# Softmax attention of block 0 with a second, transposed score product

## The chip, the cores and the metric

One core of a Trainium2 chip runs the kernel. Its engines work side by side and wait for one another by semaphores: TensorE (PE, with its weight loads as PEld), VectorE (DVE), ScalarE (ACT), GpSimd (POOL), and SyncE (SP), which issues most transfers. The metric is the time of one execution in microseconds (us). The kernel before takes 4012.47 us, the median of 3 runs (4009.18 to 4015.44). A difference of 0.2%, 8 us, is about what a measurement of this kernel can tell from no change.

## The reference

64 sequences of 128 tokens, width 256, go through two transformer blocks. The change is in the two attentions of the first block ("block 0"): 16 heads of width 16, one self-attention and one cross-attention over 128 context rows of width 192.

```python
def _attn(q, k, v):          # 16 heads of 16
    scores = jnp.einsum('bhnd,bhmd->bhnm', q, k) * HD ** (-0.5)
    p = jax.nn.softmax(scores, axis=-1)
    return jnp.einsum('bhnm,bhmd->bhnd', p, v)      # then heads joined

h = _ln(x, ln1_w, ln1_b) * (1 + sc1) + sh1
q, k, v = jnp.split(h @ Wqkv + bqkv, 3, axis=-1)
x = x + _attn(q, k, v) @ Wos + bos
h = _ln(x, ln2_w, ln2_b) * (1 + sc2) + sh2
x = x + _attn(h @ Wq + bq, context @ Wk + bk, context @ Wv + bv) @ Woc + boc
h = _ln(x, ln3_w, ln3_b) * (1 + sc3) + sh3
x = x + gelu(h @ W1 + b1) @ W2 + b2
...                          # block 1: two attentions with heads of 64, one FFN
```

## The kernel before

**Passes and ticks.** The work is six passes over all 64 sequences: two attentions of block 0 (kind "a", passes 0 and 1), its FFN (pass 2), two attentions of block 1 (kind "b", passes 3 and 4), its FFN (pass 5). Within a pass the sequences go in 16 groups of 4; one sequence is called a batch here. The function `schedule` (L127) puts every stage of every batch at a tick, a step of an imaginary clock that all engines go through in the same order. Each engine's program is one loop over the ticks, and within a tick it runs its stages in the order in which the code has them. So the order on each engine is fixed; how long a tick lasts is up to the waits. Passes 0 and 1 take 4 ticks a batch, 16 a group.

**fp32r triples.** Products that need fp32 accuracy are made of three fp32r products (`three`, L617 to L624): each operand is split into a high part (rounded to fp32r) and a low part, and high x high, high x low and low x high add up in one PSUM bank. Products of plain fp32 operands are written as one `matmul`; the trace shows each as two MATMUL records.

**One batch in passes 0 and 1.** q and k of a group are projected with head and channel on the partitions (L705, L713) and split: AH and AL for q, KBH and KBL for k; k is stored twice, times a mask that keeps one head of each pair. The heads lie in four row groups of 32 partitions. `scores0` (L690 to L703) makes, for one half of a batch (two row groups), twelve fp32r products of 256 columns, with queries on the partitions of the result, in PSUM banks 0 and 1 or 2 and 3. The DVE takes the maxima (`max0`, L1065). ACT computes exp(score - max) with the maximum as its per-partition bias and sums each row by the way (`exp0`, L926): 16 instructions of 128 columns a batch, each with an accumulator read. The DVE takes 1/sum (L1078), POOL multiplies (`normal`, L1265), PE turns each of the four tiles with four transposes (`p_turn`, L816), and DVE (three tiles, L1073) and ACT (one, L958) copy them into PT. Then `pv0` (L748) multiplies with V, ACT and DVE split the result into OH and OL (L917, L1125), and `out0` makes the output projection, which `res0` (L1106) adds to X.

**PSUM.** Banks 0 to 3 hold the scores. Everything else takes turns through banks 4 to 7 (`Banks`, L89): each use waits until the use before it in that bank has been read.

**Names.** `s_s0` counts score halves, `s_nm0` maxima, `s_exp` exponentials, `s_t` turned tiles, `s_ol` split outputs. `q.wait_ge(semaphore, value)` makes an engine wait.

## Time and profile before

| | before |
|---|---|
| median of 3 runs | 4012.47 us |
| the profiled execution | 4010.95 us |
| its span, first to last instruction | 4009.1 us |
| PE, DVE, ACT, POOL busy | 3839.5, 3157.0, 2468.4, 2862.1 us (96, 79, 62, 71%) |
| granted TensorE clock, mean | 0.993 |

The table's busy shares are means over six passes of three kinds. Passes 0 and 1 end near 1200 us, the FFN of block 0 near 1560 us, block 1's attentions near 3620 us. A stage is read from windows that lie wholly inside it. L numbers are lines of the kernel before. PE records have modelled ends: a matmul's duration contains a tail that the next one overlaps, so what a group of matmuls costs is read from its start to the start of what follows.

### The profile page before, as it was taken

How to read it: one execution, taken by the hardware profiler on the slowest of the kernel's cores; microseconds unless marked ns; L12 is line 12 of the kernel's file. 1: busy time of each engine (PE TensorE's matmuls, PEld its weight loads, DVE VectorE, ACT ScalarE, POOL GpSimd, SP SyncE). 2: the span in 40 equal slices, each digit the busy share in tenths (PEclk: the TensorE clock that was granted, in tenths of full speed). 3: DMA queues.
4: the chain of work that ended last, by engine and by line, in shares of the span. 5: the costliest groups of instructions: out<-in, count | busy, mean ns of one | idle time of the engine just before them, and what ended most of it. 6: DMA issues, size and time to landing. Idle time of an engine off the chain costs nothing.

```text
span 4009.1 us, 92934 instructions
## 1 busy us (share of the span) xinstructions
PE 3839.5 (96%) x32822; PEld 3295.7 (82%) x32822; DVE 3157.0 (79%) x6610; ACT 2468.4 (62%) x10244; POOL 2862.1 (71%) x2674
## 2 busy tenths in 40 slices
PE   7999999999989999999999999899999999999999
PEld 6777777777779997888888888788888888878998
DVE  7888889899985557888888888799998999975443
ACT  6999998898883334555555555455555555554333
POOL 5777877777767777666666666577777777766776
PEclk9999999999999999999999999999999999999999
DMA  2011111111111123777767677777777777772110
GB/s 81 28 33 33 33 46 41 41 49 49 54 40 54 43 64 102 219 210 219 216 212 223 208 222 225 215 213 235 223 231 222 226 231 225 231 227 85 52 43 32
DMA packets 415216, 544.98 MB, mean 136 GB/s; under 512 B 58524, under 2 KB 311968, under 8 KB 414752
## 3 DMA queue, kind: packets, MB, share of 16 engines
q1 hardware_dynamic: 267228, 404.74, 30.7%
q10 hardware_dynamic: 147524, 134.30, 12.9%
q8 instruction: 261, 4.28, 0.5%
q14 instruction: 203, 1.66, 0.1%
HBM read 220.11 MB, written 184.55 MB: 101 GB/s over the span
## 4 chain that ended last, share of the span: by engine, by line
PE 69%; DVE 12%; ACT 8%; DMA 4%; issue 3%; POOL 3%; ACTq 1%; SPq 0%; DVEq 0%
PE BANKS L621 17%; PE BANKS L622 15%; PE BANKS L623 15%; PE BANKS L780 6%; PE BANKS L768 5%; ACT PR L926 5%; PE BANKS L701 3%; PE BANKS L816 3%; DMA PB<-p_scratch 2%; DMA p_scratch<-TR 2%; PE BANKS L838 2%; DVE WL L1118 1%; DVE PT L1073 1%; POOL PR L1265 1%; DVE SN L1146 1%
## 5 line engine op out<-in xcount | busy, mean ns | idle before, releaser
L1265 POOL TENSOR_TENSOR PR<-PR,RL 128x512 f32<-128x512 f32 x1024 | 1064.1, 1042 | 602.9 <-DVE RL L1078 602.5
L942 ACT ACTIVATE PR<-BANKS,NM 128x128 f32<-128x128 f32 x2048 | 719.3, 378 | 334.5 <-DVE NM L1132 333.9
L926 ACT ACTIVATE PR<-BANKS,NM 128x128 f32<-128x128 f32 x2048 | 728.7, 414 | 12.7 <-DVE NM L1065 10.5
L621 PE MATMUL BANKS<-HH,WH 128*128 128x512 f32 x1632 | 681.4, 418 | 9.1 <-issue 7.4
L622 PE MATMUL BANKS<-HL,WH 128*128 128x512 f32 x1632 | 643.4, 394 | 0.0
L623 PE MATMUL BANKS<-HH,WL 128*128 128x512 f32 x1632 | 642.5, 394 | 0.0
L926 ACT ACTIVATION_READ_ACCUMULATOR PR<-BANKS,NM 128x1 f32 x2048 | 521.3, 255 | 0.0
L933 ACT ACTIVATE OH<-BANKS 128x512 fp32r<-128x512 f32 x256 | 153.1, 598 | 499.6 <-PE BANKS L768 257.8
L1132 DVE TENSOR_REDUCE NM<-BANKS 128x8 f32<-128x1024 f32 x256 | 310.4, 1213 | 190.4 <-PE BANKS L780 190.3
L942 ACT ACTIVATION_READ_ACCUMULATOR PR<-BANKS,NM 128x1 f32 x2048 | 445.5, 218 | 0.0
L621 PE MATMUL BANKS<-WH,OH 128*128 128x256 f32 x1280 | 375.6, 293 | 25.0 <-DVE OL L1150 20.8
L1277 POOL TENSOR_TENSOR HL<-HF,HH 128x512 fp32r<-128x512 f32 x192 | 256.3, 1335 | 171.0 <-DVE HH L1026 157.0
L621 PEld LDWEIGHTS BANKS<-HH,WH 128*128 128x128 f32 x1632 | 308.4, 189 | 84.1 <-issue 11.1
L969 ACT ACTIVATE HF<-BANKS,MODB,MODS 128x128 f32<-128x128 f32 x768 | 305.4, 487 | 115.5 <-PE BANKS L838 104.4
L816 PE MATMUL BANKS<-ID,PR 128*128 128x128 f32 x2048 | 316.9, 278 | 57.5 <-DVE OL L1125 22.0
L623 PEld LDWEIGHTS BANKS<-HH,WL 128*128 128x128 f32 x1632 | 308.3, 189 | 69.2
L622 PE MATMUL BANKS<-WL,OH 128*128 128x256 f32 x1280 | 359.9, 281 | 0.0
L1073 DVE COPY PT<-BANKS 128x512 f32<-128x512 f32 x384 | 262.9, 685 | 122.1 <-PE BANKS L816 121.0
L623 PE MATMUL BANKS<-WH,OL 128*128 128x256 f32 x1280 | 359.1, 281 | 0.0
L1085 DVE STREAM_TRANSPOSE TR<-PR 128x512 f32<-128x512 f32 x512 | 348.5, 681 | 10.3 <-POOL PR L1265 10.3
L1146 DVE TENSOR_TENSOR SN<-BANKS,ROPE 128x512 f32<-128x512 f32 x512 | 346.9, 677 | 6.1 <-DMA SW<-SN 5.9
L622 PEld LDWEIGHTS BANKS<-HL,WH 128*128 128x128 f32 x1632 | 309.3, 189 | 43.8
(134 smaller groups left out, 10692.2 us busy)
## 6 DMA issues: line engine op xcount, KB each, us to landing
SW<-SN SPq DMA_DIRECT2D x1024, 128.0 KB, 2.9
p_scratch<-TR SPq DMA_DIRECT2D x256, 512.0 KB, 4.7
PB<-p_scratch ACTq DMA_DIRECT2D x1024, 128.0 KB, 3.8
x_scratch<-X SPq DMA_DIRECT2D x80, 512.0 KB, 3.2
X<-x_scratch SPq DMA_DIRECT2D x80, 512.0 KB, 4.3
CX<-in_ctx SPq DMA_DIRECT2D x32, 384.0 KB, 4.4
X<-in_x SPq DMA_DIRECT2D x16, 512.0 KB, 4.0
out<-X SPq DMA_DIRECT2D x16, 512.0 KB, 2.9
```

The costliest lines, as they stand in the source:

```text
L621: e.matmul(o, lh, rh, start=first and i == 0, stop=False)
L622: e.matmul(o, lh, rl, start=False, stop=False)
L623: made = e.matmul(o, ll, rh, start=False, stop=last and i == n - 1)
L816: made = e.transpose(bank[:, 128 * h:128 * h + 128], PR[npr(t)[0]][:, 128 * h:128 * h + 128], ID[:, :])
L926: made = e.activation(pr[:, r], bank[:, r], ACT.Exp, bias=nm[:, h:h + 1], accum_out=RL[npr(t)[0]][:, h:h + 1])
L942: made = e.activation(pr[:, r], bank[:, r], ACT.Exp, bias=nm[:, h:h + 1], accum_out=RL[npr(t)[0]][:, h:h + 1])
L969: made = e.activation(HF[u % 2][:, x.c, r], bank[:, r], ACT.Identity, bias=MODB[:, s, x.c, bb:bb + 1], scale=MODS[:, s, x.c, bb:bb + 1])
L1073: e.tensor_copy(PT[npt(t)[0]][:, :], PS[tp.bank(("p", t.n))][:, :]).then_inc(s_pt_d, 1)
L1085: e.transpose(TR[i % NTR][:, :].rearrange("p (j k c) -> p j k c", j=4, k=8)[:, :, 4 * e_:4 * e_ + 4, :], PR[npr(t)[0]][:, :].rearrange("p ...
L1132: e.tensor_reduce(NM[x.i % 2][:, :], BANKS[:, 2:4, :].rearrange("p e (h k) -> p (e h) k", h=4), AX, ALU.max, negate=True).then_inc(s_nm, 1)
L1146: e.tensor_tensor(SN[r % 2][:, :].rearrange("p (b t) -> p b t", b=G), src, sn, ALU.mult).then_inc(s_rt, 1)
L1265: e.tensor_tensor(p3, p3, RL[npr(t)[0]][:, :].unsqueeze(2).broadcast_to([128, 4, 128]), ALU.mult).then_inc(s_nrm, 1)
```

## The change

Passes 0 and 1 compute their softmax in another way; block 1 and the FFNs stay as they are.

- **Operands.** q and k are no longer split. QB is q times the mask (twice, one for each head of a pair), KF is k, both plain fp32. The bias of k is added by ACT (the products with BK and ONES are gone).
- **First score product, for the maxima.** `scores` makes eight plain fp32 products of 128 columns a half, always in banks 0 and 1.
- **The maxima get onto the partitions that are contracted.** POOL splits the 16 maxima of a batch into high and low (`top`), PE turns them in one transpose (`top_turn`), and the DVE spreads them with a mask into M (`top_out`).
- **Second score product.** Six ticks later `turned_scores` makes the same scores with keys on the partitions (four plain fp32 products of 256 columns a half, banks 2 and 3), and `turned_tops` adds minus the maximum through four fp32r products of 256 columns with a matrix of zeros and ones (SEL). On PE both halves are issued as one block: the scores of one half and the turned scores of another half, which always lies in the other two row groups.
- **exp** is then one ACT instruction of 512 columns per tile, four a batch, without bias and sum, and writes PT itself. `normal`, `p_turn` and the PT copies are gone.
- **Sums.** The unused columns of V hold 1.0 instead of 0.0, so `pv0` (same count of products, now each with its own output columns) also gives each head's sum. The DVE transposes the result in 32x32 blocks (`sums`) and takes the reciprocals, POOL scales it (`scale0`, two instructions), the DVE transposes it back (`back`), ACT and POOL split it (`high0`, `low0`).
- **Ticks.** `pv0` comes 10 ticks after the batch's first score tick instead of 8 (and the first score tick is 2 later), `out0` 15 instead of 10. Group loads, norms, turns, q and k are later, nearer to their use. Three empty ticks stand between passes 1 and 2, and W2 is split later.

```diff
-                for stage, tick in (("v", tb - 3), ("v_out", tb - 2), ("pv0", tb + 8), ("high0", tb + 9), ("low0", tb + 9),
-                                    ("out0", tb + 10), ("res0", tb + 11)):
-                for u in range(4):
-                    for stage, lag in (("exp0", 0), ("normal", 1), ("p_turn", 3), ("p_copy", 4)):
+                for h in range(2):
+                    for stage, lag in (("scores0", 0), ("max0", 1), ("turned0", 6), ("exp0", 7)):
+                        at[stage, tb + 2 * h + lag].append(y)
+                for stage, lag in (("v", -3), ("v_out", -2), ("top", 4), ("top_turn", 5), ("top_out", 5), ("pv0", 10), ("sums", 11), ("scale0", 12),
+                                   ("back", 13), ("high0", 13), ("low0", 14), ("out0", 15), ("res0", 16)):
...
+            def scores(x, c, e_):
+                for r in (2 * x.h, 2 * x.h + 1):
+                    rows = slice(32 * r, 32 * r + 32)
+                    made = e.matmul(PS[r % 2][:, 256 * c + 128 * e_:256 * c + 128 * e_ + 128], QB[ga % 2][rows, c, e_, s], KF[ga % 2][rows, c, s],
+                                    start=True, stop=True)
+            def turned_scores(y, c):
+                for r in (2 * y.h, 2 * y.h + 1):
+                    e.matmul(PS[2 + r % 2][:, 256 * c:256 * c + 256].rearrange("p (e n) -> p e n", e=2), KF[ga % 2][rows, c, s], QB[ga % 2][rows, c, :, s],
+                             start=c == 0, stop=False)
+            def turned_tops(y, c):
+                    made = e.matmul(PS[2 + r % 2][:, 256 * c:256 * c + 256].rearrange("p (e n) -> p e n", e=2), SEL[rows, c, :], M[y.i // 2 % 2][rows, :, :],
+                                    start=False, stop=c == 1)
...
-                    q.wait_ge(s_exp, 4 * (4 * ga + x.b) + 2 * x.h - 2)
-                        for k, (qt, kt) in enumerate(((AH, KBH), (AH, KBL), (AL, KBH))):
-                                made = e.matmul(PS[r][:, 256 * c:256 * c + 256].rearrange("p (e n) -> p e n", e=2), qt[ga % 2][rows, c, s],
-                                                kt[ga % 2][rows, c, :, s], start=k == 0, stop=k == 2)
+                    q.wait_ge(s_nm0, x.i)
+                for y in turned:
+                    q.wait_ge(s_m, y.i // 2 + 1)
+                    q.wait_ge(s_exp, 2 * y.i)
+                for c in range(2):
+                    for x in halves:
+                        scores(x, c, 0)
+                    for y in turned:
+                        turned_scores(y, c)
+                    for x in halves:
+                        made = scores(x, c, 1)
...
-                for t in at["p_turn", tick]:
-                        made = e.transpose(bank[:, 128 * h:128 * h + 128], PR[npr(t)[0]][:, 128 * h:128 * h + 128], ID[:, :])
...
-                        made = e.activation(pr[:, r], bank[:, r], ACT.Exp, bias=nm[:, h:h + 1], accum_out=RL[npr(t)[0]][:, h:h + 1])
+                    for r in (2 * x.h, 2 * x.h + 1):
+                        e.activation(PT[(4 * (x.i // 2) + r) % NPT0][:, :], PS[2 + r % 2][:, :], ACT.Exp).then_inc(s_exp, 1)
...
+                    e.transpose(TO[vi % 2][:, :, :, :, :].rearrange("p c e q d -> p (c e q d)"), PS[tp.bank(("pv", x))][:, :]).then_inc(s_to, 1)
+                        made = e.reciprocal(RC[vi % 2][:, :, e_, :], TO[vi % 2][:, :, e_, :, 16 - 16 * e_])
...
+                    e.tensor_tensor(M[vi % 2][:, :, :], PS[tp.bank(("top", x))][:, 0:128].unsqueeze(1).broadcast_to([128, 2, 128]),
+                                    MASK[:, 2:4].unsqueeze(2).broadcast_to([128, 2, 128]), ALU.mult).then_inc(s_m, 1)
...
+                    e.tensor_copy(top[:, :, 0:4], nm).then_inc(s_toph, 1)
+                    e.tensor_tensor(top[:, :, 4:8], nm, top[:, :, 0:4].bitcast(F), ALU.subtract).then_inc(s_topl, 1)
```

On PE, in a tick with a score half of pass 1, before (HH.. are projections; L701 scores, L748 `pv0`, L816 `p_turn`):

```order
L701 MATMUL BANKS<-WH,AH 128x256 x2
L701 MATMUL BANKS<-WL,AH 128x256 x2
L701 MATMUL BANKS<-WH,AL 128x256 x2
L748 MATMUL BANKS<-PT,V 32x128 [waits s_res,s_pt_a]
L748 MATMUL BANKS<-PT,V 32x128 x15
L816 MATMUL BANKS<-ID,PR 128x128 [waits s_nrm]
```

The same place after (L666 scores, L675 turned scores, L682 the maxima's products, L743 `pv0`; QBH is the buffer of QB, s_m tells that M is there):

```order
L666 MATMUL BANKS<-KF,QBH 128x128 [waits s_exp,s_m,s_nm0]
L666 MATMUL BANKS<-KF,QBH 128x128
L675 MATMUL BANKS<-QBH,KF 128x256 x2
L666 MATMUL BANKS<-KF,QBH 128x128 x4
L675 MATMUL BANKS<-QBH,KF 128x256 x2
L666 MATMUL BANKS<-KF,QBH 128x128 x2
L682 MATMUL BANKS<-M,SEL 128x256 x4
L743 MATMUL BANKS<-PT,V 32x128 [waits s_res]
L743 MATMUL BANKS<-PT,V 32x128 x15
```

The transposes behind `pv0` are gone, and the block in front of it holds two kinds of fp32 products in turn, with one set of waits ahead of all.

On DVE, two ticks of pass 1 before (L1065 maxima, L1073 PT copy, L1125 split of the output, L1097 V):

```order
L1065 TENSOR_REDUCE NM_1<-BANKS 128x8 [waits s_s0]
L1073 COPY PT<-BANKS 128x512 [waits s_t]
L1078 RECIPROCAL RL<-RL 128x4 [waits s_exp]
L1125 TENSOR_TENSOR OL<-BANKS,OH 128x256 [waits s_oh]
L1073 COPY PT<-BANKS 128x512 [waits s_pv0,s_t]
```

And after (L1079 maxima, L1086 and L1103 block transposes, L1136 residual, L1096 M):

```order
L1079 TENSOR_REDUCE NM_1<-BANKS 128x8 [waits s_s0]
L1086 STREAM_TRANSPOSE TO<-BANKS 128x512 [waits s_pv0]
L1089 RECIPROCAL RC<-TO 128x2x4 [waits s_to]
L1089 RECIPROCAL RC<-TO 128x2x4
L1136 TENSOR_TENSOR X<-BANKS,X 128x256 [waits s_bias,s_y]
L1079 TENSOR_REDUCE NM_0<-BANKS 128x8 [waits s_topl,s_s0]
L1096 TENSOR_TENSOR M<-BANKS,MASK 128x256 [waits s_ts,s_tt]
L1103 STREAM_TRANSPOSE OF<-NO 128x256 [waits s_ol,s_no]
```

The copies of PT are gone; M is made right behind the maxima of the next batch's first half.

## Rows read from the trace of the kernel before

**Rows 1.** Windows: PE, PEld, DVE, ACT, POOL busy us (instructions), clock, DMA share, GB/s.
```profile
255.10:533.90 278.80, 262.19 (x2962) 221.59 (x2961) 236.66 (x545) 258.16 (x1203) 221.38 (x225) 1.00 0.10 32
750.80:1039.50 288.70, 264.14 (x2978) 221.96 (x2977) 261.82 (x586) 259.09 (x1203) 221.30 (x225) 1.00 0.15 45
1240.00:1560.00 320.00, 317.70 (x2068) 288.07 (x2067) 170.09 (x368) 117.26 (x224) 235.21 (x205) 1.00 0.18 58
```

**Rows 2.** Waits in 255.1 to 533.9: waiter, cause, total us, times, longest us.
```profile
PEld BANKS L701 <- ACT PR L926: 11.7, 24, 0.7
```

**Rows 3.** Timeline of PE, 402 to 411 us: start, duration, what, count.
```profile
402.32 0.60 PE L816 MATMUL BANKS<-ID,PR 128*128 128x128 f32 x4
402.68 0.48 PE L621 MATMUL BANKS<-HH,WH 128*128 128x512 f32 x1
...
404.15 0.60 PE L816 MATMUL BANKS<-ID,PR 128*128 128x128 f32 x4
404.68 0.38 PE L701 MATMUL BANKS<-WH,AH 32*128 32x256 f32 x2
...
405.58 1.08 PE L748 MATMUL BANKS<-PT,V 128*32 128x128 f32 x32
406.59 0.66 PE L816 MATMUL BANKS<-ID,PR 128*128 128x128 f32 x4
407.00 0.37 PE L621 MATMUL BANKS<-WH,HH 128*128 128x256 f32 x1
...
407.80 0.60 PE L816 MATMUL BANKS<-ID,PR 128*128 128x128 f32 x4
408.55 0.39 PE L701 MATMUL BANKS<-WH,AH 32*128 32x256 f32 x2 [0.15 <-ACT PR L926]
...
410.63 0.48 PE L723 MATMUL BANKS<-ONES,BK 128*128 128x512 f32 x1
410.95 0.40 PE L621 MATMUL BANKS<-HH,WH 128*128 128x512 f32 x1
```

**Rows 4.** Timeline of PE near 2002 us, block 1's plain fp32 scores.
```profile
2001.59 1.16 PE L780 MATMUL BANKS<-KT,QT 64*128 64x128 f32 x16
2002.68 0.50 PE L621 MATMUL BANKS<-HH,WH 128*128 128x512 f32 x1
```

**Rows 5.** Timeline of PE near 36.7 us, the first two score halves.
```profile
36.63 0.38 PE L701 MATMUL BANKS<-WH,AH 32*128 32x256 f32 x4
36.85 0.28 PE L701 MATMUL BANKS<-WL,AH 32*128 32x256 f32 x4
36.97 0.28 PE L701 MATMUL BANKS<-WH,AL 32*128 32x256 f32 x4
```

**Rows 6.** Groups by line, 255.1 to 533.9 us: busy us, mean ns | idle before.
```profile
L926 ACT ACTIVATE PR<-BANKS,NM 128x128 f32<-128x128 f32 x514 | 182.8, 413 | 0.0
L1265 POOL TENSOR_TENSOR PR<-PR,RL 128x512 f32<-128x512 f32 x129 | 133.9, 1044 | 56.8 <-DVE RL L1078 56.8
L1065 DVE TENSOR_REDUCE NM<-BANKS 128x8 f32<-128x1024 f32 x64 | 77.5, 1211 | 0.0
L1073 DVE COPY PT<-BANKS 128x512 f32<-128x512 f32 x96 | 65.9, 686 | 39.7 <-PE BANKS L816 39.1
L1324 POOL TENSOR_TENSOR X<-X,TB 128x256 f32<-128x256 f32 x32 | 23.6, 738 | 0.0
L1118 DVE SCALAR_TENSOR_TENSOR WL<-BANKS,MASK,WH 128x512 fp32r<-128x512 f32 x32 | 22.5, 746 | 1.4
L1078 DVE RECIPROCAL RL<-RL 128x4 f32<-128x4 f32 x128 | 21.4, 167 | 0.0
L1300 POOL TENSOR_TENSOR RS<-VE,MH 128x4 f32<-128x4 f32 x8 | 8.3, 1037 | 0.7
```

**Rows 7.** Groups by line, DVE, 1600 to 3600 us: block 1's 32x32 block transposes.
```profile
L1085 DVE STREAM_TRANSPOSE TR<-PR 128x512 f32<-128x512 f32 x500 | 340.4, 681 | 10.3 <-POOL PR L1265 10.3
```

**Rows 8.** Groups by line, ACT, from 1400 us: the FFN's Gelu from PSUM.
```profile
L985 ACT ACTIVATE GF<-BANKS,COL 128x512 f32<-128x512 f32 x55 | 37.9, 689 | 102.2 <-PE BANKS L623 102.2
```

338 lines of the change are left out of this document (173 added, 165 removed).

## The prediction

> **What bounds the kernel now.** I read the windows first. In a steady stretch of pass 0 (32 batches, 278.8 us, so 8.71 us a batch) ACT is busy 258.16 us, 93%, and PE 262.19 us, 94%; POOL has 79%, DVE 85%. In pass 1 (32 batches in 288.7 us, 9.02 us a batch) PE has 91%, DVE 91% and ACT 90%: three engines in lockstep. In the FFN PE reaches 99% (317.7 of 320 us) [rows 1]. Then the waits: PE's score weights wait for ACT's exponentials, 11.7 us in 24 waits of the pass 0 stretch [rows 2]. So in pass 0 ACT sets the pace, with PE close behind. Two passes of 64 batches are 128 x 8.87 = 1135 us; that is all that the change can touch, 28% of the span.
>
> **What PE loses.** From its start to the start of what follows, a turned tile (L816) takes 402.68 - 402.32 = 0.36, 404.68 - 404.15 = 0.53, 407.00 - 406.59 = 0.41 and 408.55 - 407.80 less 0.15 idle = 0.60 us [rows 3]: 1.90 us a batch. The bias product L723 takes 410.95 - 410.63 = 0.32, one for two batches: 0.16. A score half (L701) takes 405.58 - 404.68 = 0.90; two are 1.80. Together 3.86. PE's busy time a batch is 262.19/32 = 8.19 in pass 0 and 264.14/32 = 8.25 in pass 1 [rows 1]; 4.33 and 4.39 stay.
>
> **What PE gets.** The price of plain fp32 stands in block 1: eight products of 128 columns in two row groups (16 records, L780) take 2002.68 - 2001.59 = 1.09 us to the next start [rows 4]. Of this about 0.2 is the change-over to the next kind of product: L701's twelve products go out in six pairs 0.12 apart (36.97 after 36.85), 0.70, and need 0.90 [rows 3, 5]. So eight plain products are 0.89. The new block has exactly eight of 128 columns in two row groups, and four of 256 columns, the same work, in the other two: 0.89 each, and four fp32r products of 256 columns, two pairs at 0.12, 0.23. Do the two 0.89 lie beside each other? Rows 5 answer this: the first two halves' products start four at a time, at 36.63, 36.85 and 36.97, two of each half. The program has all twelve of the second half behind the first half's twelve, yet its first ones start beside the seventh and eighth. Row groups run as streams of their own, and a stream that is behind doesn't hold up the others. The block then costs 0.89 + 0.23 + 0.2 = 1.33 (sum 1.32, rounded up), 2.66 a batch. Its other end is no overlap at all: 0.89 + 0.89 + 0.23 + 0.2 = 2.21, 4.42 a batch. I take 1.33: rows 5 show the same row groups and banks in fp32r. The turned maxima are one transpose: 0.09 (a quarter of the shortest group) to 0.6 (a whole group), I take 0.26. `pv0` keeps its 16 products (1.01 us, 405.58 to 406.59 [rows 3]). The kept 4.33 plus 2.92 is 7.25 a batch in pass 0, and 7.31 in pass 1.
>
> The Trainium skill, page "TensorE: Matmul & The Clock Gate", section "Part 3: Packing small matmuls - row/col tiling", has products of different row groups run together but says that matmuls start and end strictly in program order. By that rule the alternating short and long products of the block could hold one another up. The trace disagrees where it can be seen (36.63, rows 5); what the rule would make of the block is the first rival below.
>
> **The other engines.** ACT: L926's 182.8/32 = 5.7 us a batch go (its accumulator reads too), and one PT copy [rows 6]; four exponentials of 512 columns, one and a half q and k copies at 0.69 each [rows 8] come, 3.8, against two such copies before. 8.07 becomes about 5: far from the bound. DVE: 236.66/32 = 7.40, less three PT copies (65.9/32 = 2.06), two k splits (0.70) and four reciprocals (0.67) [rows 1, 6] is 3.97; to come are a 512-column transpose at 0.68 [rows 7], one of 256 (half, 0.35), M (256 columns from PSUM, half of a 0.69 copy and a start, 0.4) and two small reciprocals (0.33): 1.8, so 5.8; in pass 1 8.18 becomes 6.6. The transpose reads PSUM, which L1085 doesn't: L1073 reads 512 columns of PSUM in 0.686, so I add nothing. POOL: 6.92 less L1265's 4.18 is 2.74 [rows 1, 6]. To come are the two small `top` instructions, two scalings of 128 columns and a split of 256. 256 columns cost 0.738 and 512 cost 1.044 [rows 6], a line with 0.43 at zero and 0.58 at 128: 0.43 x 2 + 0.58 x 2 + 0.85 for the split (between the two rows) = 2.9, in sum 5.6. No row shows a strided scaling or so small a copy; the upper end is 1.04 for each of the five (as L1300, 4 elements): 7.9. So PE is the bound, and it is the only engine near it.
>
> **Waits that come in.** Ahead of a block PE waits for the maxima of the half before (s_nm0), for M and for the exponentials. Everything on PE stands behind it: `pv0`, projections, turns. In a tick pair with M: maxima 1.21 us [rows 6] and a hop of 0.2, then M 0.4 and a hop, about 1.95 after the first scores end. PE has, until the next block, the maxima's products (0.23), the transpose, v (0.8, 407.00 to 407.80 [rows 3]) and in three batches of four a q, k or turn: 1.3 us alone, 1.7 to 2.7 with those. So one or two waits of a few tenths a group. With exponentials: 2 x 0.69 and a hop, 1.6, behind at least 1.8 of work in the other tick pair. The hop of 0.2 is an estimate, of the size of PE's change-over. I allow 0.3 us idle a batch in pass 0 and 0.4 in pass 1, where DVE has 86%; before it was 8.71 - 8.19 = 0.52 and 0.77. The periods become 7.55 and 7.71.
>
> **The sum.** Pass 0: (8.71 - 7.55) x 64 = 74 us. Pass 1: (9.02 - 7.71) x 64 = 84 us. The way through a batch is longer (15 ticks to `out0`, not 12), and three empty ticks precede the FFN; W2's split and two Gelu rows come between the last exponentials. The last batch's chain after its scores (two blocks, four exponentials, `pv0`, DVE, POOL, DVE, ACT, POOL, about 11 us by the prices above) is covered in part by the first FFN products: I add 8 us, between 0 and 20. Span 4009.1 - 158 + 8 = 3859; around it lie 4010.95 - 4009.1 = 1.9 us, so 3861. The median of the runs is 1.5 above the profiled execution: **3862 us**.
>
> Bounds of this case: if the block's change-over costs nothing (0.4 a batch less) and PE idles only as in the FFN (1%), a batch takes 6.92 and 6.98, so 245 us go instead of 158: 3775. If idle stays as before (0.52 and 0.77, 0.3 more on the mean) and each block costs 0.3 more: 3862 + 128 x 0.3 + 128 x 0.6 = 3977.
>
> **Rivals.**
> - *No overlap in the block* (slower). Place: the alternation L666, L675 on PE. A block costs 2.21; a batch 4.33 + 4.42 + 0.26 + 0.1 idle = 9.11 in pass 0 and 9.17 in pass 1, which is 0.40 and 0.15 more than before: so 4012 + 35 + 8 = 4055. It decides from a block of about 1.95 us on ((8.71 - 4.33 - 0.26 - 0.2)/2). For it: no row shows plain fp32 in four row groups, nor unequal lengths beside each other. Against it: rows 5. This is the result that the page's rule gives.
> - *POOL becomes the bound.* With its upper end, 7.94 busy and 0.2 idle, 8.14 a batch, (0.57 + 0.88) x 64 = 93 us go and 8 come: 4012 - 85 = 3927. For it: L1300's 4 elements take 1.04 [rows 6]. Against: that is one operation (a power), all others shrink with size.
> - *The change doesn't shorten the stage because the chains do the pacing*: score, maxima, M, next block. If each tick pair took 1.95 + 1.33 + 1.0 of delay by DVE's order, a batch takes 8.6, 1.0 more than forecast: 3862 + 128 = 3990, hardly faster. For it: DVE runs `back` and M in order behind the maxima, and `back` waits for POOL. Against: DVE has 14% or more free.
>
> **Chances.** Forecast case 0.75; POOL 0.08; chains 0.07; no overlap 0.08; the rest (something between the blocks' two ends, near 4012) 0.02. The range 3780 to 3970 holds most of the forecast case (its own bounds are 3775 and 3977) and the POOL case, and leaves out the chain's and the slower one. Faster by over 0.2% (8 us, what a measurement can tell): 0.89; within: 0.03; slower: 0.08.
>
> **What would show it.** In a timeline of PE, L666 and L675 records start together (four at a time) and the block from first start to `pv0` takes about 1.3 us; 2.2 would be the rival. Windows inside pass 0 should give PE about 95% and ACT about 65%, with 7.5 us a batch. POOL at 70 to 75%, its small instructions at 0.3 to 0.6 us; `top` at 1 us would speak for the second rival. DVE's L1086 at 0.7 us. A wait of PE for DVE's M over 0.5 us a batch would show the chain. Block 1 and the FFNs must keep their times; a change there would be an error of this reading.

## The result and the profile after

The changed kernel takes 3900.89 us (median of 4 runs, 3897.50 to 3902.93), the one before 4013.95 us beside it: ratio 0.9716, interval 0.9698 to 0.9733. Forecast were 3862 us and a range of 3780 to 3970. The sign and the range held; 39 us of the forecast gain did not come. The profiled execution took 3901.6 us, its span is 3899.6 us.

The span cut at the starts of the same records in both traces (the maxima, L1079 after and L1065 before, and the Gelus, L999 after and L985 before) shows where:

| stage | before | after | change | forecast |
|---|---|---|---|---|
| start to first maximum | 41.77 | 39.86 | -1.9 | 0 |
| pass 0: to the 129th maximum | 563.10 | 483.42 | -79.7 | -74 |
| pass 1: to the last maximum | 570.66 | 513.42 | -57.2 | -84 |
| change-over: to the 17th Gelu | 60.06 | 77.38 | +17.3 | +8 |
| FFN, 96 Gelus | 278.96 | 282.32 | +3.4 | 0 |
| block 1: to the 129th Gelu | 2110.95 | 2115.21 | +4.3 | 0 |
| second FFN, to the end | 383.62 | 388.00 | +4.4 | 0 |

Windows of the changed kernel, 32 batches of pass 0, 32 of pass 1, and FFN; they answer to [rows 1], with the same columns (PE, PEld, DVE, ACT, POOL busy, clock, DMA share, GB/s):
```profile
222.30:460.20 237.90, 230.34 (x3492) 194.19 (x3488) 181.94 (x400) 138.49 (x272) 150.78 (x257) 1.00 0.13 39
653.70:915.50 261.80, 240.76 (x3508) 200.42 (x3504) 207.17 (x441) 140.26 (x272) 150.63 (x257) 0.97 0.17 50
1130.00:1316.00 186.00, 186.00 (x1205) 169.67 (x1204) 93.40 (x211) 65.79 (x127) 133.84 (x119) 1.00 0.14 46
```
In pass 0 a batch takes 237.90/32 = 7.43 us, PE is busy 97% of it and ACT 58%, no longer 93%. Pass 1 is another picture: 8.18 us a batch, PE at 92%, and a mean clock of 0.97.

The block itself, in the timeline of PE (start, duration, what, count, idle before it):
```profile
402.40 0.38 PE L666 MATMUL BANKS<-KF,QBH 32*128 32x128 f32 x2
402.42 0.48 PE L675 MATMUL BANKS<-QBL,KF 32*128 32x256 f32 x2
402.59 0.42 PE L666 MATMUL BANKS<-KF,QBH 32*128 32x128 f32 x4
...
403.20 0.47 PE L682 MATMUL BANKS<-M,SEL 32*128 32x256 f32 x2
403.26 0.30 PE L666 MATMUL BANKS<-KF,QBH 32*128 32x128 f32 x2
403.50 0.28 PE L682 MATMUL BANKS<-M,SEL 32*128 32x256 f32 x2
403.85 1.08 PE L743 MATMUL BANKS<-PT,V 128*32 128x128 f32 x32
```
Scores (L666) and turned scores (L675) start 0.02 apart and run beside each other. This one takes 1.45 us to the start of `pv0`. Of the 43 blocks between 260 and 420 us the median is 1.31 us from the first start to the start of what follows; forecast was 1.33.

Groups by line in the same stretch of pass 0 (busy us, mean ns | idle before), which answer to [rows 6] and [rows 7]:
```profile
L1079 DVE TENSOR_REDUCE NM<-BANKS 128x8 f32<-128x1024 f32 x64 | 78.1, 1221 | 28.4 <-PE BANKS L666 28.3
L923 ACT ACTIVATE PT<-BANKS 128x512 f32<-128x512 f32 x128 | 69.6, 597 | 59.7 <-PE BANKS L682 59.7
L1287 POOL TENSOR_TENSOR NO<-TO,RC 128x128 f32<-128x128 f32 x64 | 24.5, 403 | 7.9 <-DVE RC L1089 7.9
L1295 POOL TENSOR_TENSOR OL<-OF,OH 128x256 fp32r<-128x256 f32 x32 | 23.4, 730 | 39.5 <-ACT OH L947 39.5
L1086 DVE STREAM_TRANSPOSE TO<-BANKS 128x512 f32<-128x512 f32 x32 | 22.9, 715 | 1.3
L1096 DVE TENSOR_TENSOR M<-BANKS,MASK 128x256 fp32r<-128x256 f32 x32 | 13.4, 420 | 14.3 <-PE BANKS L751 14.3
L1280 POOL TENSOR_TENSOR TOP<-NM,TOP 128x16 fp32r<-128x16 f32 x32 | 7.2, 225 | 2.6
L1278 POOL CAST TOP<-NM 128x16 fp32r<-128x16 f32 x32 | 6.4, 200 | 10.8 <-DVE NM L1079 10.8
```
ACT's exponentials went from 182.8 us [rows 6] to 69.6, and they now wait for PE. POOL's two small `top` instructions cost 0.20 and 0.23 us, not 0.43 and never 1.04, so the rival in which POOL is the bound has nothing left: POOL has 150.78/32 = 4.7 us a batch, forecast were 5.6.

What is wrong in pass 1 stands once in every group in the timeline of PE:
```profile
785.13 0.28 PE L639 MATMUL BANKS<-WL,HH 128*128 128x256 f32 x1
786.85 0.44 PE L860 MATMUL BANKS<-ID,Z 128*128 128x128 f32 x2 [1.45 <-ACT HF L982]
787.60 0.66 PE L871 MATMUL BANKS<-ID,CX 128*128 128x128 f32 x4 [0.31 <-DVE HL L1232]
...
790.26 1.92 PE L743 MATMUL BANKS<-PT,V 128*32 128x128 f32 x32
```
A `turn` waits 1.45 us until ACT has read another one out of its PSUM bank, a `c_turn` 0.31 for DVE. ACT is late by the new chain: in its timeline the read (L982) stands behind `high0` (L947), and this one has waited for DVE's `back` (L1103).
```profile
785.69 0.42 ACT L947 ACTIVATE OH<-OF 128x256 fp32r<-128x256 f32 x1 [0.66 <-DVE OF L1103]
786.01 0.79 ACT L982 ACTIVATE HF<-BANKS,MODB,MODS 128x128 f32<-128x128 f32 x2
```
All twelve such waits between 600 and 1000 us have these 0.66 us in front. Behind PE's two waits, `pv0` takes 1.85 us to the next start (792.11) where it took 1.01 in [rows 3]. The windows ahead of the waits and behind them (columns as above):
```profile
776.00:785.00 9.00, 9.00 (x141) 7.78 (x138) 6.33 (x13) 5.95 (x12) 4.54 (x10) 1.00 0.37 121
788.60:792.10 3.50, 3.50 (x58) 2.73 (x50) 2.30 (x3) 1.08 (x2) 0.34 (x1) 0.51 0.57 150
```
PE was busy without a gap at a granted clock of 1.00, stood for 1.45 + 0.31 = 1.8 us with 0.44 of work between, and went on; from 788.5 on the granted clock fell, and each of the three microseconds from 789 to 792 has 0.50, the lower of the two levels.

At the change-over from pass 1 to the FFN, PE stands still before the FFN's first `down` (the second product of the FFN; `up` is the first). Timeline of ACT, DVE and PE:
```profile
1059.17 1.28 ACT L923 ACT_TABLE_LOAD   x1
1060.46 1.08 ACT L923 ACTIVATE PT<-BANKS 128x512 f32<-128x512 f32 x2
...
1061.87 1.28 ACT L999 ACT_TABLE_LOAD   x1
...
1063.75 1.99 ACT L1005 ACTIVATE WH<-STG 128x1024 fp32r<-128x1024 f32 x2
...
1064.83 3.57 DVE L1260 TENSOR_TENSOR WL<-STG,WH 128x1024 fp32r<-128x1024 f32 x2 [0.52 <-ACT WH L1005]
...
1068.51 0.55 PE L614 MATMUL BANKS<-WH,GH 128*128 128x256 f32 x1 [8.25 <-DVE WL L1260]
```
By the last row W2's low part, behind two changes of ACT's function table, is what `down` waits for, 8.25 us.

### The profile page after: what moved, and what is told of

It is laid out like the page before. It is cut to its first block, busy times and chain, and to the rows that moved or that the text cites. A ratio compares the mean times of both kernels' runs of the same rounds, so it can differ in the third digit from the quotient of the medians.

```text
span 3899.6 us, 92972 instructions
## 1 busy us (share of the span) xinstructions
PE 3750.1 (96%) x34934; PEld 3217.8 (83%) x34934; DVE 2930.1 (75%) x6035; ACT 1996.6 (51%) x6534; POOL 2583.4 (66%) x2803
## 4 chain that ended last, share of the span: by engine, by line
PE 79%; DVE 9%; issue 4%; POOL 3%; DMA 2%; ACT 1%; ACTq 1%; SPq 0%; DVEq 0%; POOLq 0%
PE BANKS L614 19%; PE BANKS L615 17%; PE BANKS L616 17%; PE BANKS L810 6%; PE BANKS L798 6%; PE BANKS L666 3%; PE BANKS L743 2%; PE BANKS L675 2%; POOL HL L1313 2%; PE BANKS L860 2%; PE BANKS L682 1%; DMA p_scratch<-TR 1%; DVE SN L1156 1%; DMA PB<-p_scratch 1%; PE BANKS L626 1%
## 5 line engine op out<-in xcount | busy, mean ns | idle before, releaser
L962 ACT ACTIVATE PR<-BANKS,NM 128x128 f32<-128x128 f32 x2048 | 720.9, 379 | 348.3 <-DVE NM L1142 348.0
L1301 POOL TENSOR_TENSOR PR<-PR,RL 128x512 f32<-128x512 f32 x512 | 533.0, 1041 | 335.8 <-DVE RL L1108 334.9
L1142 DVE TENSOR_REDUCE NM<-BANKS 128x8 f32<-128x1024 f32 x256 | 310.3, 1212 | 197.2 <-PE BANKS L810 197.1
L962 ACT ACTIVATION_READ_ACCUMULATOR PR<-BANKS,NM 128x1 f32 x2048 | 444.7, 217 | 0.0
L923 ACT ACTIVATE PT<-BANKS 128x512 f32<-128x512 f32 x512 | 278.3, 596 | 279.8 <-PE BANKS L682 279.1
L1079 DVE TENSOR_REDUCE NM<-BANKS 128x8 f32<-128x1024 f32 x256 | 312.7, 1221 | 108.3 <-PE BANKS L666 107.4
L982 ACT ACTIVATE HF<-BANKS,MODB,MODS 128x128 f32<-128x128 f32 x768 | 293.5, 457 | 138.8 <-PE BANKS L860 134.7
L1308 POOL TENSOR_TENSOR QT<-QT,SW 128x512 f32<-128x512 f32 x256 | 332.5, 1299 | 10.4 <-DMA SW<-SN 10.4
L1308 POOL TENSOR_TENSOR KT<-KT,SW 128x512 f32<-128x512 f32 x256 | 330.7, 1292 | 13.0 <-DMA SW<-SN 12.7
```

The lines of the kernel that those rows point to most:

```text
L962: made = e.activation(pr[:, r], bank[:, r], ACT.Exp, bias=nm[:, h:h + 1], accum_out=RL[npr(t)][:, h:h + 1])
L982: made = e.activation(HF[u % 2][:, x.c, r], bank[:, r], ACT.Identity, bias=MODB[:, s, x.c, bb:bb + 1], scale=MODS[:, s, x.c, bb:bb + 1])
L1079: e.tensor_reduce(NM0[x.i // 2 % 2][:, x.h, :, :], BANKS[:, 0:2, :].rearrange("p r (h k) -> p r h k", h=4), AX, ALU.max, negate=True).then ...
L1142: e.tensor_reduce(NM[x.i % 2][:, :], BANKS[:, 2:4, :].rearrange("p e (h k) -> p (e h) k", h=4), AX, ALU.max, negate=True).then_inc(s_nm, 1)
L1301: e.tensor_tensor(p3, p3, RL[npr(t)][:, :].unsqueeze(2).broadcast_to([128, 4, 128]), ALU.mult).then_inc(s_nrm, 1)
L1308: e.tensor_tensor(z[:, :], z[:, :], SW[r % NSW][:, :], ALU.add).then_inc(s_zz, 1)
```

## The experiments

All times are medians; "less" and "more" are against the changed kernel's 3900.9 us unless said otherwise. Ratios with their intervals are to the kernel before, run beside them (4009 to 4012 us).

**Why the block overlaps.** The changed kernel issues two score products, then two turned ones, and so on. Three runs change this order and nothing else, and a fourth adds a wait to it.

All score products first (16 records of L666), then all turned ones:
```diff
-                for c in range(2):
-                    for x in halves:
-                        scores(x, c, 0)
-                    for y in turned:
-                        turned_scores(y, c)
-                    for x in halves:
-                        made = scores(x, c, 1)
-                        if c == 1:
-                            made.then_inc(s_s0, 1)
+                for x in halves:
+                    for c in range(2):
+                        scores(x, c, 0)
+                        made = scores(x, c, 1)
+                    made.then_inc(s_s0, 1)
+                for c in range(2):
+                    for y in turned:
+                        turned_scores(y, c)
```


> The changed kernel with one thing moved: PE issues all eight score products of a half first, then the four turned products, then the tops, instead of one pair in turn with the other. Waits, products and sizes are the same. Theory (row groups run as streams of their own; a product of an idle row group starts although longer ones stand ahead of it): the block still takes about 1.45 us from its first start to pv0's, the run is within 0.3% of the changed kernel's 3900.9 us. Rival A (products start strictly in program order, and only the alternation gave the overlap): the turned ones start only when the last score product has started, about 0.7 us later, so the block takes 1.9 to 2.2 us, x 256 blocks = 120 to 190 us more: 4020 to 4090 us. Rival B (it overlaps, but the maxima can start earlier since the scores all stand ahead): up to 0.1 us a block less, 3875 to 3900 us, visible in pass 1 above all.

Measured: 4019.2 us (4014.2 to 4024.9), ratio 1.0021 (1.0009 to 1.0032): the whole gain is gone. One block in the timeline of PE (L859 is what follows):
```profile
405.75 0.82 PE L666 MATMUL BANKS<-KF,QBL 32*128 32x128 f32 x10
406.32 0.48 PE L675 MATMUL BANKS<-QBH,KF 32*128 32x256 f32 x2
406.42 0.39 PE L666 MATMUL BANKS<-KF,QBL 32*128 32x128 f32 x4
...
407.10 0.59 PE L682 MATMUL BANKS<-M,SEL 32*128 32x256 f32 x4
407.61 0.44 PE L859 MATMUL BANKS<-ID,Z 128*128 128x128 f32 x2
```
The first turned records start when ten score records have started and six have not, 0.56 us late; the block takes 407.61 - 405.75 = 1.86 us. My theory is wrong as it stands, and so is rival A, by which they would have waited for all sixteen.

All score products first, and PE waits until they are done (the edit as it stands on top of the run just shown):
```diff
+                    q.wait_ge(s_s0, x.i + 1)
                 for c in range(2):
                     for y in turned:
                         turned_scores(y, c)
```


> The changed kernel, all score products of a half first, and PE then waits for their completion before it issues the turned products, so nothing in the block overlaps. This is the price of no overlap. By the prediction's terms (0.89 more a block) the block takes 2.2 to 2.4 us, 256 x 0.8 to 0.95 = 205 to 243 us more, less where PE would have waited anyway (0.24 us a batch in pass 0, 0.66 in pass 1, 115 us at most): 4000 to 4140 us, 4090 us taken. If it comes out below 3950 us, the overlap isn't what holds the block at 1.45 us, and something else sets the block's time.

Measured: 4236.4 us (4230.1 to 4242.1), ratio 1.0566 (1.0551 to 1.0582), 335 more. In its timeline of PE:
```profile
405.10 1.16 PE L666 MATMUL BANKS<-KF,QBL 32*128 32x128 f32 x16
406.32 1.13 PE L675 MATMUL BANKS<-QBL,KF 32*128 32x256 f32 x8
407.11 0.58 PE L682 MATMUL BANKS<-M,SEL 32*128 32x256 f32 x4
407.62 0.33 PE L751 MATMUL BANKS<-ID,TOP 128*128 128x128 f32 x1
```
The block takes 2.52 us, 1.21 more than 1.31. I had it at 2.2 to 2.4: the turned ones start 1.22 after the first score product, not 0.89, since a wait for completion also sees the last product's 0.27 us to its end. 256 x 1.21 = 310 us is near the 335 by luck. Pass 0 takes 134 us more than in the changed kernel, less than 128 x 1.21 = 155, for PE's idle time shrank; pass 1 takes 206 more, 11.5 us a batch, at a mean granted clock of 0.87 (720 to 1300 us).

Coarser steps: for each c four score products (8 records), then the two turned ones.
```diff
                 for c in range(2):
                     for x in halves:
                         scores(x, c, 0)
+                        made = scores(x, c, 1)
+                        if c == 1:
+                            made.then_inc(s_s0, 1)
                     for y in turned:
                         turned_scores(y, c)
-                    for x in halves:
-                        made = scores(x, c, 1)
-                        if c == 1:
-                            made.then_inc(s_s0, 1)
```


> The changed kernel with the block's products alternating in coarser steps: for each c, first the four score products (8 records), then the two turned ones (4 records). In the run with all score products ahead (4019.2 us, 16 records ahead) the turned ones started 0.56 us after the block's start, when 10 of the 16 score records had started and 6 were still to come. Theory (a product of an idle row group may pass about six records that have not started, and no more): here only 6 records are left ahead when the first pair has started, so the turned ones start within 0.12 us of the block's start; the block takes 1.45 to 1.55 us, the run 3895 to 3925 us. Rival (a product passes only its next neighbour or two, and the time depends on how fine the alternation is): the turned ones start 0.3 us late in each c, the block takes 1.65 to 1.8 us, the run 3950 to 3990 us.

Measured: 3918.4 us (3912.1 to 3923.6), ratio 0.9764 (0.9748 to 0.9780). The turned ones start 0.03 us after the first two score records, with six ahead; the median block takes 1.43 us. The theory had 1.45 to 1.55 us and a run of 3895 to 3925.

Twelve records ahead, to test the number:
```diff
+                for x in halves:
+                    scores(x, 0, 0)
+                    scores(x, 0, 1)
+                    scores(x, 1, 0)
+                for y in turned:
+                    turned_scores(y, 0)
+                for x in halves:
+                    scores(x, 1, 1).then_inc(s_s0, 1)
+                for y in turned:
+                    turned_scores(y, 1)
```


> The changed kernel with twelve score records ahead of the first turned product in each block (then four turned records, the last four score records, the last four turned ones). It tests the look-ahead by number. Theory (a record of an idle row group starts once no more than six that have not started stand ahead): the turned ones start with the seventh and eighth score record, 0.33 us after the block's start, in the run with sixteen ahead it was with the ninth and tenth, 0.56; the block takes 1.63 us (1.31 in the changed kernel), the run 3950 to 3980 us. Rival A (the look-ahead covers a fixed time, about 0.6 us, and not a number of records): the turned ones start at 0.56 here too, or at 0. Rival B (a coarser alternation costs nothing as long as it alternates): block below 1.45 us, run below 3925.

Measured: 3963.8 us (3956.7 to 3967.8), ratio 0.9882 (0.9864 to 0.9901), block 1.63 us. In its timeline of PE:
```profile
405.50 0.60 PE L666 MATMUL BANKS<-KF,QBL 32*128 32x128 f32 x6
405.84 0.48 PE L675 MATMUL BANKS<-QBL,KF 32*128 32x256 f32 x2
```
Six score records have started when the turned ones start, at 0.34 us: six are left again. All three numbers are as expected. It is a number of records and not a fixed time. The four orders give blocks of 1.31, 1.43, 1.63 and 1.86 us and 3901, 3918, 3964 and 4019 us.

The Trainium skill, page "TensorE: Matmul & The Clock Gate", section "Part 3: Packing small matmuls - row/col tiling", has matmuls start strictly in program order. The records disagree: a pair of L675 at 406.32 starts ahead of six records of L666 that stand before it in the program. The reach is six records. It stood in the trace of the kernel before, just ahead of [rows 5]:
```profile
36.28 0.39 PE L701 MATMUL BANKS<-WH,AH 32*128 32x256 f32 x2
36.50 0.28 PE L701 MATMUL BANKS<-WL,AH 32*128 32x256 f32 x2
36.62 0.28 PE L701 MATMUL BANKS<-WH,AL 32*128 32x256 f32 x2
```
Six of the first half's twelve records had started when the second half's first pair did, at 36.63 (the pair with 0.38 us among those four; the first half's own next pair came at 36.73). Six were left there too. Those products are fp32r, one record each, and the plain fp32 ones have two, so the reach counts records and not products. I had read the rows as having no such limit.

**Who held the kernel before, ACT or PE.** First the kernel before with ACT relieved alone:
```diff
-                    for h in range(4):
-                        r = slice(128 * h, 128 * h + 128)
-                        made = e.activation(pr[:, r], bank[:, r], ACT.Exp, bias=nm[:, h:h + 1], accum_out=RL[npr(t)[0]][:, h:h + 1])
-                    made.then_inc(s_exp, 1)
+                    e.activation(pr[:, :], bank[:, :], ACT.Exp, scale=0.01).then_inc(s_exp, 1)
```


> The kernel before with ACT relieved alone: each tile's four exponentials of 128 columns with row sums become one of 512 columns without maxima and sums (left out: the maxima, the sums, and a scale of 0.01 keeps the numbers finite; the sums are ones from a fill). PE, DVE and POOL do all that they did. ACT falls from 8.07 to about 5.1 us a batch. Theory (of the prediction: PE is right behind ACT, with 8.19 to 8.25 us of busy time a batch, so ACT's relief alone is worth little, and the rest of the gain is PE's shorter work): a batch takes 8.35 to 8.6 us in both passes, so 3940 to 3985 us, a third of the change's gain at most. Rival (ACT set the pace alone, and its relief is the whole gain): 3900 us or less, 7.4 to 7.8 us a batch. Second rival (DVE and POOL in lockstep hold it): 3995 to 4010 us, no gain.

Measured: 3991.4 us (3988.4 to 3993.3), ratio 0.9948 (0.9932 to 0.9965): 20 us of 113. Its window in pass 0:
```profile
255.00:530.00 275.00, 263.86 (x2964) 222.07 (x2964) 236.13 (x545) 153.66 (x305) 221.94 (x225) 1.00 0.10 32
```
This run leaves out the maxima and the row sums of the exponentials. ACT fell to 56%, PE went from 94 to 96%, and a batch from 8.71 to 8.59 us. So in pass 0 ACT was first by little, and PE next, as the prediction said. In pass 1 a batch fell from 9.04 to 8.88 us (48 batches each) and not to 8.6; PE had 93% there and DVE 92%, so there DVE's part, the second rival, isn't ruled out. The time lies 6 us above the theory's range and 4 below this rival's.

Then the other corner, the changed kernel with dearer exponentials:
```diff
-                        e.activation(PT[(4 * (x.i // 2) + r) % NPT0][:, :], PS[2 + r % 2][:, :], ACT.Exp).then_inc(s_exp, 1)
+                        pt, bank = PT[(4 * (x.i // 2) + r) % NPT0], PS[2 + r % 2]
+                        for k in range(4):
+                            s = slice(128 * k, 128 * k + 128)
+                            made = e.activation(pt[:, s], bank[:, s], ACT.Exp, accum_out=SUM[:, 4 * r + k:4 * r + k + 1])
+                        made.then_inc(s_exp, 1)
```


> The changed kernel with ACT's exponentials as dear as in the kernel before: each of 512 columns is cut into four of 128 with a row sum (into a spare tile that nobody reads), about 5.7 us a batch instead of 2.2; PE, DVE and POOL do what the changed kernel does. With the run that relieved ACT alone (3991.4 us, 20 less than before) this is the other corner. Theory (both are needed: before, ACT's 8.07 and PE's 8.2 us a batch stood side by side, so either cut alone is worth little): ACT is at 7.8 to 8.1 us a batch, a batch of pass 0 takes 8.0 to 8.3 us, of pass 1 8.3 to 8.6, the run 3940 to 3985 us. Rival (PE alone was the bound and ACT only looked like it): within 10 us of the changed kernel's 3900.9. The spare tile moves the FFN's buffers by another 64 bytes; whether its 16 down units take 46.5 or 47.05 us shows which places are the slow ones, at most 12 us of the run.

Measured: 3930.7 us (3928.5 to 3935.1), ratio 0.9807 (0.9792 to 0.9822), below the expected 3940 to 3985. Its window in pass 0, with ACT busy in the fourth place:
```profile
222.00:464.00 242.00, 224.65 (x3391) 189.48 (x3386) 177.44 (x391) 195.31 (x1134) 144.94 (x249) 1.00 0.11 37
```
ACT got only to 81%, 6.3 us a batch and not the 8 that I had meant, for without the maxima as bias an exponential took 0.295 us. So the run doesn't build the corner that it was for. Still passes 0 and 1 together took 503.35 + 540.33 = 1043.7 us against 996.8: 47 us more although ACT was not the busiest engine. The rival, within 10 us, falls: the cut on PE is worth less with ACT loaded so far. How much a fully loaded ACT would cost stays open, and with it whether the gain needs both cuts. Part of the 47 us was given back further on (below).

**Pass 1.** The context's transposes two ticks later, out of the tick in which `turn`, `top_turn` and `v` take banks too:
```diff
-                    at["c_turn", tg - 16 + c if p == 1 else tg - 7].append(Part(p, g, c, 0))
+                    at["c_turn", tg - 14 + c if p == 1 else tg - 7].append(Part(p, g, c, 0))
-                    at["c_split", tg - 15 + c if p == 1 else tg - 6].append(Part(p, g, c, 0))
+                    at["c_split", tg - 13 + c if p == 1 else tg - 6].append(Part(p, g, c, 0))
```


> The changed kernel with the transposes of the context (c_turn, pass 1) two ticks later, at tg-14 and tg-13, and their splits likewise; nothing else. In the changed kernel they fall into the two ticks where turn, top_turn and v take banks too, and PE waits once a group for ACT's HF (L860, about 1.5 us) to give a bank back, with the clock at half speed behind it. Theory (this order makes pass 1 0.7 us a batch slower than pass 0): the L860 waits on ACT go, the clock in pass 1 is back near 1.00, the period in pass 1 falls from 8.15 to 7.6 to 7.8 us a batch: 22 to 35 us less, 3866 to 3879 us. Rival (DVE with its splits of the context is what paces pass 1; 79% busy and in order): the wait goes elsewhere, less than 8 us are gained.

Measured: 3861.4 us (3858.1 to 3864.5), ratio 0.9631 (0.9618 to 0.9644), 39.5 less, a little more than expected; in the profiled executions pass 1 itself is 31.9 us shorter (513.42 to 481.51). Waits of PE in pass 1 of the changed kernel (total us, times, longest), and then its window here:
```profile
PEld BANKS L860 <- ACT HF L982: 13.2, 8, 1.7
...
PE BANKS L860 <- ACT HF L982: 11.6, 8, 1.4
```
```profile
653.70:895.50 241.80, 229.92 (x3503) 194.03 (x3496) 204.32 (x438) 138.37 (x271) 150.87 (x256) 1.00 0.18 54
```
The eight waits are gone, the clock is 1.00, and a batch takes 7.61 us (from the starts of 48 batches' maxima), 8.17 before the repair. Of these 0.56 us about half was idle time of PE and half busy time at the lower clock: a batch has 0.37 us idle and 7.24 busy here, 0.66 and 7.52 before the repair. The rival falls, for it allowed less than 8 us. But DVE, now at 85%, is what PE still waits for most in this window:
```profile
PE BANKS L666 <- DVE NM L1079: 9.1, 7, 1.3
```

**Where buffers lie.** The new small buffers go to the end of the first stage's region, 128 unused bytes take their old place, and all that follows from ID on, the FFN's buffers too, has the address that it had in the kernel before:
```diff
-        NM0 = [sb(f"NM0_{i}", [128, 2, 2, 4]) for i in range(2)]
-        RC = [sb(f"RC{i}", [128, 2, 2, 4]) for i in range(2)]
+        sb("PADS", [128, 32])
...
-        BQ = sb("BQ", [128, 2, 2, 2])
...
             TOP = [sb(f"TOP{i}", [128, 4, 32], R, stack=first) for i in range(2)]
+            NM0 = [sb(f"NM0_{i}", [128, 2, 2, 4], stack=first) for i in range(2)]
+            RC = [sb(f"RC{i}", [128, 2, 2, 4], stack=first) for i in range(2)]
+            BQ = sb("BQ", [128, 2, 2, 2], stack=first)
```


> The changed kernel with its new small buffers (NM0, RC, BQ) put at the end of the first stage's region and 128 bytes in their old place, so that all buffers from ID on, with GH, GL, OH1, OL1 among them, have the same addresses as in the kernel before. In the changed kernel they stand 128 to 160 bytes higher. Theory (the 256-column products of the FFNs and of block 1's out projection go 0.120 us apart instead of 0.117 because of where their operands lie): 16 down units take 46.5 us again instead of 47.05, passes 2 and 5 lose 4 us each and block 1 about 4: 10 to 13 us less, 3888 to 3891 us. Rival (the slower rate is of the chip's state in that execution or of something else in the program, such as its instruction addresses): 3897 to 3905 us, 16 units at 47.0.

Measured: 3887.0 us (3883.6 to 3891.6), ratio 0.9696 (0.9683 to 0.9709), 13.9 less. By the two ratios, each against the kernel before in its own session, it would be 8, and their intervals overlap; the stages are surer. The 96 Gelus take 278.96 us, to the hundredth what they took before, block 1 2110.5 and the second FFN 383.57. The first and last product of one `down` unit and the first of the next work, in the changed kernel and then in this one:
```profile
1190.54 0.29 PE L614 MATMUL BANKS<-WH,GH 128*128 128x256 f32 x1
...
1191.86 0.29 PE L616 MATMUL BANKS<-WH,GL 128*128 128x256 f32 x1
1191.99 0.60 PE L860 MATMUL BANKS<-ID,Z 128*128 128x128 f32 x4
```
```profile
1180.26 0.28 PE L615 MATMUL BANKS<-WH,GH 128*128 128x256 f32 x1
...
1181.55 0.28 PE L617 MATMUL BANKS<-WH,GL 128*128 128x256 f32 x1
1181.66 0.40 PE L615 MATMUL BANKS<-HH,WH 128*128 128x512 f32 x1
```
Twelve products: 1.45 us there, 1.40 here. Block 1 is less sure than the FFNs: in the profiled executions with the new addresses it took 2112.6 to 2117.3 us, with the old ones 2108.4 to 2113.0.

The same from the other side, the kernel before with nothing but an unused tile:
```diff
+        sb("PADS", [128, 40])
         ST = [sb(f"ST{i}", [128, G, 6]) for i in range(2)]
```


> The kernel before with 160 unused bytes ahead of ST, so that all buffers from there on stand 160 bytes higher, as GH, GL, OH1 and OL1 do in the changed kernel; no instruction differs otherwise. Putting the changed kernel's buffers back to their old addresses gave 13.9 us. Theory (it is the address alone): the FFN's 16 down units take 47.05 instead of 46.49 us, passes 2 and 5 together 8 us more, block 1 about 4 more: 4020 to 4027 us against 4011. Rival (the two things go together only in the changed kernel): 4008 to 4014 us.

Measured: 4029.7 us (4025.6 to 4034.2), ratio 1.0043 (1.0028 to 1.0058), 18 more than before, even above what I expected. 96 Gelus take 281.93 us, the second FFN 388.07. The addresses alone do it. In the run with the dearer exponentials the buffers from OH on, GH and GL among them, stand 64 bytes above those of the changed kernel and all others where they were, and there 96 Gelus take 277.63 us and block 1 2107.65, the quickest of all. So it is a buffer from OH on that matters, and no run singles one out. By the sizes of the tiles added up in each kernel, GH starts 96 bytes beyond a multiple of 128 in the kernel before, at a multiple in the changed and the padded kernel, the slow place, and 64 beyond in the quickest run. That the rule lies in the rest by 128 is a guess from three places; a kernel with the best of them and the repairs was not run.

**The change-over.** W2's first half split before the last exponentials, the FFN two ticks later with its first norms where they were, two `up` products issued early, Gelu only behind the last exponential, and `down` waiting for its half alone:
```diff
-    T0[_p + 1] = END[_p] + {1: 3, 2: 2, 4: 0}.get(_p, 0)
+    T0[_p + 1] = END[_p] + {1: 5, 2: 2, 4: 0}.get(_p, 0)
...
                     at["up", tg + j].append((p, g, j))
+                    at["up_mm", tg + j - ((3, 2)[j] if (p, g) == (2, 0) and j < 2 else 0)].append((p, g, j))
...
-    chunks += [(e1 - 17, "W1", 0), (e1 - 13, "W1", 1), (e1 + 5, "W2", 0), (e1 + 5, "W2", 1)]
+    chunks += [(e1 - 17, "W1", 0), (e1 - 13, "W1", 1), (e1 + 4, "W2", 0), (e1 + 6, "W2", 1)]
...
-                    q.wait_ge(s_wlo, w_ready[WFF[p][1]])
+                    q.wait_ge(s_wlo, w_ready[WFF[p][1], j // 4])
```


> The changed kernel with the change-over from pass 1 to the FFN reordered: W2's first half is split before the last exponentials, its second half behind the second Gelu, the first two up products of the FFN are issued among the last batches, Gelu runs only behind the last exponential (one table change instead of three), and down waits only for the half of W2 that it reads. In the changed kernel PE idles 8.25 us ahead of the first down, with the clock at half speed before and behind it, and from the last maximum to the 17th Gelu it takes 77.4 us (60.1 before). Theory (that wait ends with W2's split, which stands behind two table changes and Gelu on ACT): the wait shrinks to 1 to 3 us, 77.4 becomes 67 to 72, and the run 3891 to 3896 us. Rival (the chain of the last batch is what PE waits for, W2 ends only by chance last): less than 2 us gained, 3899 to 3902 us.

Measured: 3898.0 us (3895.0 to 3906.6), ratio 0.9718 (0.9703 to 0.9732), 3 less and within what the runs can tell. The one wait became another, in the timeline of PE:
```profile
1064.16 0.58 PE L615 MATMUL BANKS<-WH,OH 128*128 128x256 f32 x1 [4.77 <-POOL OL L1296]
```
The stretch took 73.8 us. It took 74.5 to 75.7 in the eight other runs that left it alone, so the 77.4 of the changed kernel's profile was a high draw, and this order is worth about 1 us.

**Both repairs together,** the context's transposes two ticks later and the buffers at their old addresses:

> Both repairs together: the context's transposes two ticks later (alone 3861.4 us, 39.5 less than the changed kernel) and the buffers back at their old addresses (alone 3887.0, 13.9 less). They touch different stages, so the gains should add: 3900.9 - 39.5 - 13.9 = 3847.5 us, 3844 to 3852. If it is above 3855, one of them worked through something that the other also mends.

The edits are those of the two repairs. Measured: 3850.3 us (3845.5 to 3853.4), ratio 0.9593 (0.9580 to 0.9606): 50.6 less, where 39.5 + 13.9 = 53.4 were to be had. They add. This is the quickest version with the fewest edits, 161.9 us under the kernel before.

**Both repairs and a second form of the change-over,** shown against its first form (the FFN's first norms keep their ticks again):
```diff
-    T0[_p + 1] = END[_p] + {1: 5, 2: 2, 4: 0}.get(_p, 0)
+    T0[_p + 1] = END[_p] + {1: 6, 2: 2, 4: 0}.get(_p, 0)
...
-    chunks += [(e1 - 17, "W1", 0), (e1 - 13, "W1", 1), (e1 + 4, "W2", 0), (e1 + 6, "W2", 1)]
+    chunks += [(e1 - 17, "W1", 0), (e1 - 13, "W1", 1), (e1 + 4, "W2", 0), (e1 + 7, "W2", 1)]
...
-                    at["up_mm", tg + j - ((3, 2)[j] if (p, g) == (2, 0) and j < 2 else 0)].append((p, g, j))
+                    at["up_mm", tg + j - ((4, 3)[j] if (p, g) == (2, 0) and j < 2 else 0)].append((p, g, j))
```


> The two repairs and a second form of the reordered change-over from pass 1 to the FFN. The first form (3898.0 us, 3 less than the changed kernel, 77.4 to 73.8 us from the last maximum to the 17th Gelu) still left PE waiting 4.8 us, for POOL's OL of the second last batch, which stood on POOL behind the FFN's first GL, and this behind ACT's table change. Here Gelu and GL come one tick later, behind that OL. Theory (order on POOL was what PE waited for): the stretch falls to 68 to 72 us, the run is 3 to 8 us under the one with the two repairs: 3840 to 3845 us. Rival (the latency of the last batches' chain, with no further score products beside it, is the bound whatever the order): within 3 us of it.

Measured: 3850.4 us (3847.8 to 3854.0), ratio 0.9596 (0.9583 to 0.9609), no different from the run with the two repairs; the stretch took 74.5 us in both. My theory on the change-over falls for good: the first other order moved PE's wait from DVE's WL to POOL's OL, the second broke it into several of 1.2 to 2.0 us for POOL's GL and OL, and the length stayed. That the last batches' own chain sets it is what is left, and only argued; no run shortened that chain.

## Why the prediction held, and where it did not

- *The block costs 1.33 us.* Measured 1.31. The number was right and half of the reason wrong: "a stream that is behind doesn't hold up the others" holds only for six records ahead. The forecast came true because the program alternates; in another order of the same products the change would have been worth nothing (4019 us). So far as the order goes this was luck, for [rows 5], from which I took the rule, already had six records left where the overlap began.
- *The first rival, no overlap, 2.21 us and 4055 us.* It did not happen. Forced by a wait the block is 2.52 us and the kernel 4236 us, but part of that block is the wait for the last product's end, which the rival doesn't have: the turned ones start 1.22 us after the block's start where they could have started at 0.89, with the last score product, or at 1.00, one step of 0.11 behind it. That leaves 2.2 to 2.3, near 2.21. So its block was priced about right; the 4055 us leave out what a slower clock in pass 1 would add, and no run shows the rival as it was meant. What does happen in a bad order lies between: 1.86 us and 4019.
- *PE's busy time, 7.25 and idle 0.3 in pass 0.* Measured 230.34/32 = 7.20 and 0.24, a batch 7.43 for 7.55. Pass 0 gave 80 us, forecast 74.
- *The other engines.* ACT 138.49/32 = 4.3 (forecast 5), DVE 181.94/32 = 5.7 (5.8), in pass 1 6.5 (6.6), POOL 4.7 (5.6). None became the bound.
- *Pass 1, 7.71 a batch.* Failed: 8.18. The step "one or two waits of a few tenths a group" missed one of 1.45 us, which comes not from the new block but from the order in which the four PSUM banks are taken. The change did two things there: it added `top_turn` as a user, and it moved `turn` from 24 to 21 ticks ahead of its group to 18 to 15 ticks, onto the two ticks of `c_turn` (16 and 15). By the kernel's order the `turn` that waits is then the fourth use after the `turn` before it, with `c_turn`, `top_turn` and `v` between, so it gets the same bank, and ACT reads this bank behind its own 0.66 us wait. Moving `c_turn` ends it; which of `top_turn`, the moved `turn` and ACT's order weighs how much no run separates. The wait then cost the clock, 0.97 on the mean: PE's busy time rose to 240.76/32 = 7.52 for a forecast of 7.31. With the transposes moved the batch takes 7.61 us. This is 27 of the 39 us.
- *The change-over, +8.* Measured +17 in that execution and about +15 in the others, inside my 0 to 20. My covering of the last batch's chain by the first FFN products was too hopeful; what ends it is open.
- *Block 1 and the FFNs keep their times.* Failed: 3.4 + 4.3 + 4.4 = 12 us more, from the addresses of operands. I had said that a change there would be an error of this reading, and it was: I read no addresses out of the diff, which enlarges small buffers ahead of everything.
- *ACT sets the pace before, PE close behind.* Right for pass 0: ACT relieved alone gave 20 us of 113, 10 in each pass. In pass 1 DVE's part stays open.

## What to carry to other kernels

Small products of different row groups overlap when the program interleaves them finely; have no more than six records of the busy row groups left ahead of the first of the idle ones, and read the distance from the first starts in the timeline, not from the busy share. When a change adds a user to a rotating set of PSUM banks or moves one to another tick, count the uses tick by tick: one wait of 1.5 us a group cost twice, the second time through the clock. Put new small buffers behind the old ones, or compare the spacing of untouched products before and after, since a shift by bytes moved stages that the change never named.

## What the runs showed of the hardware that I had not expected

- The reach of six: with 16, 12 and 8 records of two row groups ahead, the first record of the two other row groups started after 10, 6 and 2 of them, at 0.56, 0.34 and 0.03 us, the same in every block of pass 0 whose records are all in the trace. Six were left in each, and six of twelve fp32r records at 36.63 us in the kernel before.
- Where operands lie changes the rate of fp32r products of 256 columns: `down` units of 1.45 and 1.40 us, 96 FFN units in 282.3, 279.0 or 277.6 us by the place.
- On POOL a copy of 16 columns takes 0.20 us and a strided scaling of 128 columns 0.40 us, beside 1.04 us for a power of 4 elements [rows 6]: the kind of operation weighs more than its size.
- An exponential of 128 columns without a bias took 0.295 us against 0.413 with one [rows 6], each with its row sum.
